# Latent attention: GpSimd adds the two rotated parts of each head's own query tile, and TensorE takes one product per head

## The reference, cut to what matters

```python
q_hk  = (hidden_q @ Wq.T).reshape(Bv, Sv, H, K)               # K = 128
q_big = jnp.einsum('bshk,hkq->bshq', q_hk, w_kc_q)            # 192 rows a head
q_big = q_big * cos_q + _rotate_half(q_big) * sin_q           # halves of 96 swapped
kv_r  = _apply_rope(kv_c, sin_k, cos_k)                       # 64
q_r   = jnp.einsum('bshq,hqr->bhsr', q_big, W_qr)             # 192 -> 64
k_r   = jnp.einsum('bld,hdr->bhlr', kv_r, W_kr)
attn  = softmax(jnp.einsum('bhsr,bhlr->bhsl', q_r, k_r))
ctx_c = jnp.einsum('bhsl,bld->bhsd', attn, kv_r)
ctx   = jnp.einsum('bhsd,hkd->bhsk', ctx_c, w_kc_kv)
return ctx.reshape(Bv, Sv, H * K) @ Wo.T
```

## Time and profile before

| | |
|---|---|
| median of 3 runs | 845.84 us (844.61 to 846.84) |
| the profiled execution: its time, its span | 842.39 us, 840.6 us |
| TensorE busy in the span | 726.7 us (86%) |
| DVE, ACT, POOL busy | 579.1, 430.0, 199.8 us |
| the changed stage | from 112.5 to 433 us |
| first `packed` product, last `add` | 128.42 us, 433.04 us |

### The profile page before, as it was taken

How to read it: one execution, slowest core, us unless ns; L and a number is a source line. 1 busy time by engine, 2 the same in 40 slices (tenths; PEclk the granted TensorE clock), 3 DMA queues, 4 the chain that set the end, 5 groups by cost and what they waited for, 6 DMA issues and landing times. The chain is left out here.

```text
span 840.6 us, 13322 instructions
## 1 busy us (share of the span) xinstructions
PE 726.7 (86%) x4826; PEld 468.9 (56%) x4826; DVE 579.1 (69%) x1107; ACT 430.0 (51%) x894; POOL 199.8 (24%) x298
## 2 busy tenths in 40 slices
PE   6999968898999989898857469999489999759998
PEld 3555655566666666666533245666334444357887
DVE  5678567675767676676749964565668999565666
ACT  5468632635455363635549665455266767432332
POOL 2422020303030220303043514120121111361350
PEclk9999979999999999999988779999859999969999
DMA  4634313111112021110124006120010333302111
GB/s 129 175 99 131 125 33 86 59 30 47 42 33 75 1 75 29 47 29 14 26 74 111 27 8 178 50 77 2 15 43 21 82 74 82 100 2 98 55 51 50
DMA packets 49760, 52.24 MB, mean 62 GB/s; under 512 B 10116, under 2 KB 40388, under 8 KB 49588
## 3 DMA queue, kind: packets, MB, share of 16 engines
q1 hardware_dynamic: 45718, 50.37, 21.6%
q10 hardware_dynamic: 3978, 1.02, 0.6%
HBM read 26.58 MB, written 2.04 MB: 34 GB/s over the span
## 5 line engine op out<-in xcount | busy, mean ns | idle before, releaser
L522 DVE TENSOR_REDUCE a_nm<-ps 128x2 f32<-128x512 f32 (+1 forms) x112 | 75.3, 688 | 28.1 <-PE ps L818 19.4
L2538 DVE TENSOR_REDUCE x_nm<-ps 128x2 f32<-128x512 f32 x128 | 84.9, 686 | 12.3 <-PE ps L2679 9.9
L2623 ACT ACTIVATE x_pt<-ps 128x1024 f32<-128x1024 f32 x64 | 62.5, 1021 | 34.4 <-PE ps L2707 33.7
L1583 PE MATMUL ps<-m_xp,m_mp 128*128 128x512 f32 x288 | 73.9, 397 | 1.0 <-DVE m_wr L1306 1.0
L1458 ACT ACTIVATE m_junk<-ps,m_nm 128x256 bf16<-128x256 f32 x128 | 58.6, 484 | 30.2 <-DVE m_nm L1318 30.2
L1270 POOL TENSOR_SCALAR fw<-fw,finv 128x256 f32<-128x256 f32 x24 | 11.6, 482 | 245.2 <-PE ps L1661 245.2
L2679 PE MATMUL ps<-kx,a_qs 96*128 96x256 bf16 x256 | 53.0, 296 | 8.2 <-DMA a_qs<-a_ks 6.6
L1583 PEld LDWEIGHTS ps<-m_xp,m_mp 128*128 128x128 f32 x288 | 51.8, 189 | 14.1 <-issue 3.1
L3054 PE MATMUL ps<-x_xp,x_wp 128*128 128x512 f32 x216 | 54.6, 403 | 0.1
L1286 DVE TENSOR_TENSOR m_qcs<-ps,mw_tab 64x512 f32<-64x512 f32 x64 | 44.1, 688 | 8.9 <-PE ps L1583 7.1
L3054 PEld LDWEIGHTS ps<-x_xp,x_wp 128*128 128x128 f32 x216 | 40.4, 193 | 8.9 <-issue 0.3
(11 more groups left out here) (305 smaller groups left out, 1711.0 us busy)
## 6 DMA issues: line engine op xcount, KB each, us to landing
a_qs<-a_parts SPq DMA_DIRECT2D x48, 128.0 KB
a_ks<-a_parts SPq DMA_DIRECT2D x48, 128.0 KB
m_q<-m_qs SPq DMA_DIRECT2D x32, 128.0 KB
x_gb<-scr_g SPq DMA_DIRECT2D x8, 512.0 KB, 3.7
fw<-in_f_w SPq DMA_DIRECT2D x12, 256.0 KB
a_qs<-a_ks SPq DMA_DIRECT2D x48, 64.0 KB
mw_wq<-in_m_wq SPq DMA_DIRECT2D x8, 256.0 KB, 2.8
mw_wo<-in_m_wo SPq DMA_DIRECT2D x8, 256.0 KB, 2.8
```

Source lines behind the costliest of these rows:

```text
L522: dve.tensor_reduce(dst, src, AX.X, ALU.max, negate=True).then_inc(mx_done.sem, 1)
L1583: mm = pe.matmul(c.ps[:, QB_BANKS[k], :], mp[:, p % 2, w, dt, tile * P:(tile + 1) * P], xp[:, x, dt, half_cols(half)], start=((dt, w, x) = ...
L2538: dve.tensor_reduce(nm[:, n % ITEMS, QT * u:QT * u + QT], c.ps[:, u % 2, :].rearrange("p (t k) -> p t k", t=QT), AX.X, ALU.max, negate=Tru ...
L2623: act.activation(pt[:, n % 2, kt, :], c.ps[:, 2 + 2 * kt:4 + 2 * kt, :].rearrange("p b n -> p (b n)"), ACT.Exp, scale=SCALE).then_inc(exp_ ...
```

## The change

An own tile's two parts are now added before TensorE sees them. DVE writes the sin products with the two halves of 64 partitions swapped (two products of 64 rows where one of 128 stood), then the cos product over all 128. POOL adds the sin part onto the cos part in place (`own_tile`, 128 x 512), and scored_own takes one product a head instead of two. For this the rows of a tile lie differently: an own tile now holds 64 rows of each half of the head (0 to 63 and 96 to 159), the shared tile the last 32 of each half, of both heads. So fold writes each of its four products in two parts (128 and 64 columns), the weights need four sets of 64 columns instead of six (absorb, absorbed_weights), ACT copies the turned weights in four pieces instead of three, and the table is loaded by seven DMAs instead of one, two tiles wide instead of three. Four additions a pair go onto POOL's list ahead of its ternary work, and a counter (`whole`) tells TensorE of them.

```diff
-        sp.dma_start(self.tab[:, :, :, :], self.io["rope_q"]).then_inc(self.tab_in.sem, 16)
+        for tile, (to, rows, source) in ((0, (0, 64, (0, 0))), (0, (64, 32, (0, 96))), (0, (96, 32, (1, 0))),
...
+            sp.dma_start(self.tab[to:to + rows, :, tile, :], self.io["rope_q"][first:first + rows, :, k, :])\
+                .then_inc(self.tab_in.sem, 16)
...
+                def own_tile(p, half, h):
+                    pool.wait_ge(rope.sem, rotated(p, 3 * half + 2 + h))
+                    turned_part = qcs[:, half, OWN_TILES[h], 1, :]
+                    plain = qcs[:, half, OWN_TILES[h], 0, :]
+                    pool.tensor_tensor(plain, plain, turned_part, ALU.add).then_inc(whole.sem, 1)
+
+                own_tile(0, 0, 0)
                 for p in range(PAIRS):
+                    own_tile(p, 0, 1)
+                    own_tile(p, 1, 0)
+                    own_tile(p, 1, 1)
+                    if p + 1 < PAIRS:
+                        own_tile(p + 1, 0, 0)
                     pool.wait_ge(stt.sem, 4 * p + 2)
...
-                    for cs in range(2):
+                    for part in range(2):
                         dve.tensor_tensor(
-                            qcs[:, half, tile, cs, :].rearrange("p (b q) -> p b q", q=SEQ),
-                            c.ps[:, QB_BANKS[k], :].rearrange("p (b q) -> p b q", q=SEQ),
-                            tab[:, cs, tile, :].unsqueeze(1).broadcast_to([P, 2, SEQ]), ALU.mult)\
+                            qcs[rows(1 - part), half, tile, 1, :].rearrange("p (b q) -> p b q", q=SEQ),
+                            c.ps[rows(part), QB_BANKS[k], :].rearrange("p (b q) -> p b q", q=SEQ),
+                            tab[rows(part), 1, 0, :].unsqueeze(1).broadcast_to([R, 2, SEQ]), ALU.mult)\
                             .then_inc(rope.sem, 1)
+                    dve.tensor_tensor(
+                        qcs[:, half, tile, 0, :].rearrange("p (b q) -> p b q", q=SEQ),
...
-                                      c.ps[:, bank, 0:6 * R], 1.0, None, ALU.mult).then_inc(wr_done.sem, 1)
+                                      c.ps[:, bank, 0:4 * R], 1.0, None, ALU.mult).then_inc(wr_done.sem, 1)
...
-                            mm = pe.matmul(c.ps[:, 6 + dt, h * DCQ:(h + 1) * DCQ], wq2[:, h, dt * P:(dt + 1) * P],
-                                           wkq[:, h, :], start=True, stop=True)
+                            by_half = wkq[:, h, :].rearrange("p (s n) -> p s n", s=2)
+                            own, shared = ((0, P), (P, DCQ)) if h == 0 else ((DCQ + R, 2 * DCQ), (DCQ, DCQ + R))
+                            for (a, b), part in ((own, by_half[:, :, 0:OWN]), (shared, by_half[:, :, OWN:])):
+                                mm = pe.matmul(c.ps[:, 6 + dt, a:b], wq2[:, h, dt * P:(dt + 1) * P], part,
+                                               start=True, stop=True)
...
-                    for j in range(2):
-                        for tile in range(3):
-                            h = (0, j, 1)[tile]
...
+                    for slot in range(4):
...
-                    pe.wait_ge(rope.sem, rotated(p, 3 * half + 3))
-                    for cs in range(2):
-                        for h, tile in ((0, 0), (1, 2)):
-                            mm = pe.matmul(c.ps[rows(h), 4 + half, :], wr[:, p % 2, cs, tile, :],
-                                           qcs[:, half, tile, cs, :], start=False, stop=(cs == 1),
-                                           skip_group_check=True)
+                    pe.wait_ge(whole.sem, whole.at(4 * p + 2 * half + 2))
+                    for h in range(2):
+                        mm = pe.matmul(c.ps[rows(h), 4 + half, :], wr[:, p % 2, OWN_SLOTS[h], :],
+                                       qcs[:, half, OWN_TILES[h], 0, :], start=False, stop=True,
+                                       skip_group_check=True)
```

More of the change, by code:

```diff
@@ L1148, in mla_stage @@
                                                  c.mla.wkv, c.mla.wo)
-        wrT, wkrT = sb("wrT", [P, 6, P]), sb("wkrT", [P, 2 * CTX])
-        wr = sb("wr", [P, 2, 2, 3, R])
+        wrT, wkrT = sb("wrT", [P, 4, P]), sb("wkrT", [P, 2 * CTX])
+        wr = sb("wr", [P, 2, 4, R])
         mp = sb("mp", [P, 2, 2, DT, 2 * DCQ], F32R)
@@ L1175, in mla_stage @@
         xp_hi, xp_lo = c.counter("at_in3"), c.counter("at_in4")
-        zeroed, tern = c.counter("at_m5"), c.counter("at_m4")
+        zeroed, tern, whole = c.counter("at_m5"), c.counter("at_m4"), c.counter("at_m6")
         w_a, w_k, w_n, tab_in = c.mla.w_a, c.mla.w_k, c.mla.w_n, c.mla.tab_in
@@ L1191, in mla_stage @@
         projected, added = c.counter("mo_y"), c.counter("mo_x")
-        EV = 5
+        EV = 6
         TILE_ORDER = (1, 0, 2)
-        WR_SLOTS = ((0, 2), (1, 4), (5, 3))
+        OWN_SLOTS, SHARED_SLOTS = (0, 3), (1, 2)
+        OWN_TILES = (0, 2)
+        OWN = P // 2
         QB_BANKS = (0, 1, 2, 3, 0, 1)
@@ L1205, in rotated @@
         def rotated(p, k):
[L1207 removed]
+            return 20 * p + 10 * (k // 3) + (0, 4, 7)[k % 3]
         HT = TT // 2
@@ L1427, in turned_weights @@
                     dst = wrT[:, :, :].rearrange("p t n -> p (t n)")
[L1428 to L1435, removed]
+                    turned_in = ps[:, 0:2 * DCQ].rearrange("p (h s n) -> p h s n", h=2, s=2)
+                    act.activation(dst.rearrange("p (k s n) -> p k s n", k=4, s=2)[:, 0:4:3, :, :],
+                                   turned_in[:, :, :, 0:OWN], ACT.Copy).then_inc(turned_ev.sem, 1)
+                    act.activation(dst[:, P:P + 2 * DCQ].rearrange("p (h n) -> p h n", h=2)[:, :, 0:R]
+                                   .rearrange("p h (s n) -> p h s n", s=2),
+                                   turned_in[:, :, :, OWN:], ACT.Copy).then_inc(turned_ev.sem, 1)
+                    swapped = dst[:, DCQ:DCQ + P].rearrange("p (h s n) -> p h s n", h=2, s=2)
+                    for k in range(2):
+                        act.activation(swapped[:, :, 1 - k, :], turned_in[:, :, k, OWN:], ACT.Copy)\
+                            .then_inc(turned_ev.sem, 1)
                     for h in range(2):
@@ L1559, in absorb @@
                         pe.wait_ge(mp_lo.sem, p + 1)
-                    for j in range(2):
-                        for tile in range(3):
-                            h = (0, j, 1)[tile]
-                            mm = pe.matmul(c.ps[:, bank, (3 * j + tile) * R:(3 * j + tile + 1) * R],
-                                           wrT[:, WR_SLOTS[tile][j], :], wkrT[:, rows(h)],
-                                           start=True, stop=True)
+                    for slot in range(4):
+                        mm = pe.matmul(c.ps[:, bank, slot * R:(slot + 1) * R], wrT[:, slot, :], wkrT[:, rows(slot // 2)],
+                                       start=True, stop=True)
                     mm.then_inc(absorbed.sem, 1)
@@ L1764, in mla_stage @@
                      (dn, 16 * PAIRS), (ln_done, 2 * PAIRS), (ms, 6 * PAIRS), (wn_lo, PAIRS), (tern, 9 * PAIRS),
-                     (zeroed, 2)):
+                     (zeroed, 2), (whole, 4 * PAIRS)):
             s.done(n)
```

14 lines of the change are left out of this document (10 added, 4 removed).

## The result

The changed kernel took 854.54 us (median of 4 runs, 853.5 to 856.37), the kernel before 845.23 (4 runs, 842.39 to 846.84): a ratio of 1.0121, 95% interval [1.0095, 1.0146]. The forecast of 847.5 us and the range up to 852.5 were both too low. Measured again beside the experiments the changed kernel stood at 851.04 against 842.80, 1.0093 [1.0069, 1.0117].

The account below looks back on a forecast made before the run. TensorE bounds a pair up to add 3, DVE and ACT after it; 0.7 (seven pairs) + 1.1 (last pair) - 1.0 (start) + 1.6 (clock) = 2.4, taken as 1.7, giving 847.5 us, range 842 to 852.5.

Parts of the forecast that it names:

- TensorE's and DVE's durations: Attention stage pair: TensorE 1.4 us less; DVE 0.84 more per own tile, add 3 0.45 earlier, fold_rest 0.22 later.
- the 2.2: Forecast length of fold's 16 records on TensorE, in us, out of a range from 2.1 to 2.8.
- the floor of 0.13 us a record: Start-to-start time of absorb's 64-column records, taken as a floor that fold's 128-column records hardly pass.
- POOL: POOL's additions, 1.30 us each, end before scored_own needs them: 2 us to spare for half 0, half 1 hidden.
- The start: Start of the attention stage: fewer absorb records at half clock and shorter absorbed_weights make it 1.0 us earlier.
- The net of a pair without the clock: DVE's path in the attention stage: about 0.1 us longer a pair, 0.7 in seven pairs; last pair 1.1.
- 4 x 0.4 = 1.6 us more: Longer wait before the transpose brings clock falls in six or seven of eight stretches instead of three, 0.4 us each.
- rival 1: Late clock falls lie over scores_t and the next pair's packed products: +6.3 us, 852 us; chance 0.22.
- Falls outside the scores: Named sign of being wrong: falls of TensorE's clock anywhere but over the scores.
- the 0.5 us that I had allowed around 37.4: Named sign of being right: a pair stays within 0.5 of 37.4 us while TensorE's busy time drops about 11 us.

Follow-up runs that it names:

- the fillers' two kernels: Unread products before each pair's transpose: ten a pair in the changed kernel, 843.58 us, 1.001; three (last pair ten) in the kernel before, 841.72 us, 0.9997.
- hybrid: Kernel before with the new form only for half 0 of each pair, half 1 keeping its straight sine product, without fillers: 841.87 us, 0.9986.
- before_two: Kernel before with scored_own's four products with the own tiles' sine parts left out (two a half): 840.70 us, 0.9956.

## Why the prediction was wrong, step by step

**TensorE's and DVE's durations: right.** scored_own 1.03 to 1.08 us (forecast 1.08), an own tile 2.05 (2.04), add 3 0.51 us earlier (0.45), fold_rest 0.16 later (0.22). The sine product without the swap shows the price of the split and its holding together: 0.55 us a pair. Fold took 1.89 us, below the 2.2 and even below the range from 2.1 to 2.8: the floor of 0.13 us a record was absorb's whole length over its 12 records, which counts in the last record's own length. Four records less took 0.45 off it (1.55 to 1.10), 0.11 each, and fold's sixteen start 0.118 apart. So TensorE's work shrank by 0.86 + 0.86 + 0.45 - 0.49, some 1.7 us a pair and not 1.4; a stretch with a fall has it busy 33.55 us instead of 35.34. Over the kernel its busy time fell by 5.9 us and not by 11, since more of it ran at half clock. The Trainium skill's rule ("VectorE: DVE Perf Modes", "Two Vector instructions with no wait between them") agrees with the trace: 0.72 us behind add 2 as behind each sine product, 0.61 after the cosine product.

**POOL: right**, shown by leaving its additions out. **The start: right**; from the first fold to the first packed product 15.9 us became 14.7 and 15.0.

**The net of a pair without the clock: nearly right.** Forecast +0.1 us a pair, +1.1 in the last. At full clock 37.33 against 37.35, and the last stretch with fillers 35.72 against 34.84. Over the seven stretches the fillers' two kernels differ by 260.1 - 258.9 = 1.2 us, 0.9 of it in the last and 0.4 in the fifth; the forecast was 0.6 + 1.1.

**"4 x 0.4 = 1.6 us more": the step that failed.** It was mis-sized inside the stage. The falls cost 264.5 - 260.1 = 4.4 us in the changed kernel and 259.7 - 258.9 = 0.8 before, 3.6 more and not 1.6: every stretch had a fall, and the price of one is not 0.4 but 0.3 to 0.8, the more the later it begins, and 1.6 where it reached over scores_t and the packed products. That was rival 1's mechanism, and I gave it 0.22. Its number, 852 us, is near what was measured partly by luck: it put 5.5 us more on the clock inside the stage, where 3.6 were found, and nothing behind it. Falls outside the scores were a sign of being wrong that I had named, and the stretch of 38.93, which has one, is also past the 0.5 us that I had allowed around 37.4. The last pair's rows had shown such a place, at a wait of 2.48 us, which is what the changed pairs were forecast to have.

**What lies behind the stage: left out.** I took all other stages as unchanged. The next two are 3.5 us longer in both profiles. 0.7 to 0.9 us of it is the first ScalarE instruction, which waits for a load and begins 4.3 to 4.4 us after the stage's start instead of 3.5; 2.0 us comes in the place of the long fall; the rest, 0.5 to 1.0, arises in the self attention. Fillers in the attention stage alone take 2.3 of the 3.5 back, but not in the place of the long fall: the fall lasts 17.1 us there too and the work shown above takes 13.86 us. 1.5 of the 2.3 is the first ScalarE instruction, which then begins 2.8 us after the start.

The traces show what goes with the long fall, though no run tests it. Leaving out the run with fillers in this stage: in the five profiles in which this fall began 6.6 to 7.6 us ahead of the ScalarE instruction shown first above (478.64 before), it lasted 10.2 us; in the eight in which it began 8.2 to 9.2 us ahead, 13.7 or 17.1. In the changed kernel the work is 0.8 us later by the load, and the fall is not. Why the load lands later stays open; the seven table loads are excluded. So does what of the 0.9 and 1.9 us in the first and last pieces belongs to the change.

## What to carry to other kernels

Before shortening TensorE, look at what follows: time taken out ahead of a wait only lengthens the wait, and a longer wait can cost the clock over the work behind it. Here a form with 1.7 us less TensorE work a pair was 0.9 to 1.2% slower, and became neutral when the wait was filled with products that nobody reads. Use a shorter form where TensorE bounds and the longer list of another engine has idle time; and fill most of what wait remains, but measure it: the same cure in the next stage's waits brought nothing. Here the best was the new form for half of the tiles with four fillers, 0.65% faster than before. Look too at where a fall of the clock will lie: falls of the same length cost 0.4 to 0.9 us behind the same wait.

## What the runs showed of the hardware

- TensorE's granted clock fell to 0.5 for 3.4 or 6.8 us around the transpose of a pair. Over the first seven pairs: with waits near 2.57 + 0.53 us in seven of seven, with 1.60 + 0.53 in five, with 0.73 + 0.53 in two (the kernel before) or four (hybrid, 0.70), with 1.35 + 0.53 behind five filling products in none: what had run just before the wait matters beside its length.
- The same fall of 3.4 us cost a stretch 0.4 to 0.9 us as it began 0.6 to 2.4 us behind the transpose (before_two), and the falls of the changed kernel lay at the same places in two profiles, to 0.1 us.
- float32 products of 128 and of 64 columns, alternating over 128 rows of weights, started 0.118 us apart on average (16 records in 1.89 us); those of 64 columns alone 0.11 (absorb, 12 records in 1.55 us and 8 in 1.10).
- GpSimd's addition of 128 x 512 float32 took 1.28 to 1.29 us beside VectorE's products from PSUM, and those kept their 0.69.
